# Attention outputs from rotated, transposed operands in the edge stage of a graph, attention and expert layer

## The reference, cut to what matters

```python
# gnn: edges (row, col), 4 heads of 64
e = leaky_relu(a_src.Wh[row] + a_dst.Wh[col], 0.2); e = exp(e - max(e))
h_new = segment_sum(Wh[col] * e / segment_sum(e)[row], row) + Wh
# mix: qn, kn are normalised; v1 = [1, v]
kv_mod = einsum('bhni,bhnj,bhne->bhije', kn, kn, v1/N)
kv = einsum('bhnd,bhne->bhde', kn, v1/N)
y = 0.5*einsum('bhni,bhnj,bhije->bhne', qn, qn, kv_mod) + s2*einsum('bhnd,bhde->bhne', qn, kv) + s4*vsum
out = (y[..., 1:] / y[..., :1]) @ Wproj.T + bproj
```

## Time and profile before

| | |
|---|---|
| Time, median of 3 | 3498.43 us (3497.71 to 3507.61) |
| Span of the profiled execution | 4552.4 us; no time of its own is given beside the span |
| Instructions | 80191 |
| Busy share of that span | PE 68%, DVE 61%, ACT 43%, POOL 47% |
| Transfers | 452.9 MB, mean 99 GB/s |

### The profile page before, as it was taken

The page is one execution under the profiler, slowest core; times in us unless marked ns, Lnnn a source line. Parts: engine busy times, 40 slices in busy tenths (PEclk is TensorE's granted clock), DMA queues, the critical chain, the costliest instruction groups (busy, mean ns, idle before and its releaser), DMA issues.

```text
span 4552.4 us, 80191 instructions
## 1 busy us (share of the span) xinstructions
PE 3118.0 (68%) x17657; PEld 2176.0 (48%) x17657; DVE 2760.2 (61%) x6376; ACT 1951.9 (43%) x5742; POOL 2159.7 (47%) x2438
## 2 busy tenths in 40 slices
PE   4888266666666666667777777777776444777895
PEld 2333133333333333456555555555555333666785
DVE  8999866666666666656555555565555465434322
ACT  4777133333333333344444444444444222544674
POOL 5877455455555555544444444444444532123123
PEclk8888677777887877788888888888888776988998
DMA  2222244343434434433333333333333333334344
GB/s 67 99 96 89 89 103 103 106 103 101 110 100 104 121 99 105 110 89 90 84 92 81 87 89 83 83 87 85 84 88 83 94 112 130 105 109 150 96 136 134
DMA packets 326431, 452.92 MB, mean 99 GB/s; under 512 B 79020, under 2 KB 261482, under 8 KB 326052
## 3 DMA queue, kind: packets, MB, share of 16 engines
q0 software_dynamic: 85552, 236.37, 19.0%
q1 hardware_dynamic: 217896, 194.32, 14.9%
q10 hardware_dynamic: 22860, 20.83, 1.6%
HBM read 366.49 MB, written 84.82 MB: 99 GB/s over the span
## 4 chain that ended last, share of the span: by engine, by line
PE 27%; DVE 21%; issue 20%; another core or an unknown queue 15%; DVEq 7%; ACT 5%; POOL 3%; ACTq 1%; DMA 1%; SPq 1%; POOLq 0%
PE bank L2046 8%; PE bank L2230 4%; PE bank L2242 4%; DVE room L1582 3%; PE bank L2080 3%; DVE room L1374 2%; DVEq L1541 2%; PE bank L2091 2%; DVE room L1373 2%; DVE room L1565 2%; DVE room L1535 1%; DVE room L1555 1%; PE bank L2055 1%; ACT room L1175 1%
## 5 line engine op out<-in xcount | busy, mean ns | idle before, releaser
L884 POOL DMA_INDIRECT room<-table,room x1564 | 1504.4, 962 | 1594.4 <-DVE room L1565 1127.9
L2046 PE MATMUL bank<-room 128*128 128x260 f32 x3520 | 1053.1, 449 | 472.4 <-DVE room L1565 291.2
L2046 PEld LDWEIGHTS bank<-room 128*128 128x128 f32 x3520 | 752.3, 225 | 634.4 <-issue 510.2
L1565 DVE TENSOR_TENSOR room<-room,bank 128x1024 f32<-128x1024 f32 x440 | 534.3, 1214 | 71.3 <-issue 41.1
L1582 DVE TENSOR_TENSOR room<-bank,room 128x1024 f32<-128x1024 f32 x392 | 477.5, 1218 | 162.6 <-remote 88.9
L1175 ACT ACTIVATE room<-bank 128x512 f32<-128x512 f32 (+1 forms) x588 | 252.4, 487 | 393.0 <-remote 306.0
L1555 DVE TENSOR_REDUCE room<-bank 128x32 f32<-128x128 f32 x440 | 125.2, 285 | 426.9 <-remote 263.8
L1107 ACT ACTIVATE bank<-room 128x16 f32<-128x16 f32 x440 | 80.8, 184 | 671.8 <-DVE room L1559 432.9
L1100 ACT ACTIVATE spare<-away,ones 128x512 bf16<-128x512 bf16 x440 | 317.6, 722 | 57.3 <-ACT away L1097 7.6
L2080 PE MATMUL bank<-ident,room 128*128 128x128 f32 x1764 | 298.8, 325 | 22.3 <-issue 11.1
L1115 ACT ACTIVATE bank<-room 128x96 f32<-128x96 f32 x392 | 96.4, 246 | 506.5 <-DVE room L1585 331.5
(11 more groups left out here) (321 smaller groups left out, 5010.7 us busy)
## 6 DMA issues: line engine op xcount, KB each, us to landing
spare<-rows_dram SPq DMA_DIRECT2D x440, 128.0 KB
room<-table,room POOLq DMA_INDIRECT x1564
kv_dram<-room SPq DMA_DIRECT2D x49, 324.0 KB, 2.2
room<-kv_dram SPq DMA_DIRECT2D x196, 81.0 KB
y_dram<-planes SPq DMA_DIRECT2D x119, 128.0 KB
room<-xs_dram ACTq DMA_DIRECT2D x110, 128.0 KB
q_dram<-room SPq DMA_DIRECT2D x49, 192.0 KB, 1.9
room<-q_dram SPq DMA_DIRECT2D x196, 48.0 KB
```

The source lines that it names most:

```text
L884: pool.indirect_dma_start(G[:, k.slot, u, :], None, table, bass.IndirectOffsetOnAxis(ap=ixbuf[:, k.slot, u:u + 1].bitcast(I32), axis=0)).t ...
L1565: dve.tensor_tensor(Gw[:, h, :, 0:C].rearrange("p u (h d) -> p u h d", h=GH), G[:, bass.ds(slot, 1), :, 0:C].rearrange("p a u (h d) -> p ( ...
L2046: ins = pe.matmul(pbank[1 + h][:, 0:TW], OH[:, s, u, :], Gw[:, h, u, :], start=(u == 0), stop=(u == U - 1))
```

## The change: what it does, and the diff

1. **q is stored transposed.** In stage 1 PE transposes q of tile a-2 (`turn_q`, three 128x128 transposes, after `project(a)`), ACT copies it (`copy_qt`, 256 and 128 columns), SP stores 192 KB into `qt_dram` (384 rows x 6272 tokens) instead of `q_dram`.
2. **q laps work on 512 tokens.** Thirteen groups of four laps (52 laps, the last group has one tile of 128 tokens). A lap handles one pair of heads for 512 tokens, a step two of a head's four chunks of 128 features. SP loads for each head q transposed four times (`rot_a`, 4 x 32 rows) and shifted by each distance (`rot_b`, 4 x 32 x 4 rows of 2 KB): 8 transfers and 1.25 MB per head; and per lap six transfers of 256 KB in all for the tail. DVE multiplies 2 x 512 columns per step, both inputs in SBUF, and once per lap the tail (512). The product is already what `y_part` needs: PE runs two matmuls of 512 columns per step, and one for the tail per lap. `ft_part`, `q_part`, `copy_unit` for q, and the two small feature operations for q go. The rest of the chain (`tail_part`, `normalise_y`, `add_bias`, `store_mix`) runs per token tile as before, one group later.
3. **Row scores of four steps at once.** PE `row_scores(lap)` makes them for a lap, two laps ahead, in bank 3; DVE `take_scores` reduces 512 elements once per lap into `row_sum`, in place of a reduction of 128 and an ordering wait per step. ACT's `copy_oht` runs eight steps ahead, SP's row loads one lap further ahead.
4. `one_hot` reads `iota_ps` (now bank 4) in all laps. `feat` and `feat_tail` have four buffers. `w2` is loaded by SP after the last q lap, `zeros` is cleared after the edge stage. GpSimd has more to clear before the edge stage (`ysT` 4096 elements per partition, `tail_y` 512, `tail_x` 1024 and two selects over it); its gathers are unchanged.

```diff
@@ sync: stores of stage 1 @@
-            sp.dma_start(q_dram[rows, :], qs[:, a.slot, :]).then_inc(st_out[a.slot], 16)
+        def store_qt(a):
+            sp.wait_ge(qt_copied, a.n + 1)
+            sp.dma_start(qt_dram.rearrange("(b p) n -> p b n", p=P)[:, :, bass.ds(a.n * P, P)], qts[:, a.slot, :, :]).then_inc(st_out[a.slot], 16)
...
@@ sync: loads of the q laps @@
+        def load_rot(gq, h):
+            r, w = h % 2, width(gq)
+            n = 8 * gq + h
+            if not isinstance(n, int) or n >= 2:
+                sp.wait_ge(qf_done, 2 * n - 2)
+            tok = bass.ds(gq * QW, w)
+            for d in range(4):
+                sp.dma_start(rot_a[d * MD:(d + 1) * MD, r, 0:w], qt_dram[h * XD:h * XD + MD, tok]).then_inc(unit_loaded[r], 16)
+                rows = bass.AP(qt_dram.tensor, qt_dram.offset + (h * XD + d) * NP, [[NP, MD], [4 * NP, FCH], [1, NP]])
+                sp.dma_start(rot_b[d * MD:(d + 1) * MD, r, :, 0:w], rows[:, :, tok]).then_inc(unit_loaded[r], 16)
...
+        def q_group(gq):
+            for l in range(QG):
+                n = 4 * gq + l
+                for s in range(4):
+                    load_row(At(n + (LAPS_K + 2), s, 4))
+                    if s == 0:
+                        load_tail(gq, l)
+                    if s % 2 == 0:
+                        load_rot(gq, 2 * l + s // 2)
+                    if s == 1 and (not isinstance(n, int) or n >= 7):
+                        store_mix(n - 7)
...
+        sp.wait_ge(y_step, 16 * NQG)
+        for e in range(XE):
+            sp.dma_start(w2[:, e, :, :], t["W2"][e].rearrange("(c p) n -> p c n", p=P)).then_inc(s_w4e, 16)
@@ scalar @@
+        def copy_qt(a):
...
+            act.activation(qts[:, s, 0:2, :].rearrange("p b n -> p (b n)"), pbank[0][:, 2 * P:4 * P], ACT.Copy)
+            act.activation(qts[:, s, 2, :], pbank[4 + (s + 1) % 2][:, MH * V1:MH * V1 + P], ACT.Copy).then_inc(qt_copied, 1)
...
-                if (k + 3).inside(STEPS):
-                    copy_oht(k + 3)
+                if (k + 8).inside(STEPS):
+                    if s < 3:
+                        copy_oht(k + 8)
+                    if s == 2:
+                        copy_oht(k + 9)
@@ vector @@
+        def take_scores(lap):
+            dve.wait_ge(s_made, lap + 1)
+            if not isinstance(lap, int) or lap > 0:
+                dve.wait_ge(z_done, 4 * lap)
+            dve.tensor_reduce(row_sum[:, :].rearrange("p (u n) -> p u n", n=2 * GH),
+                              score_ps[:, :].rearrange("p (u j n) -> p u n j", j=4, n=2 * GH), AX.X, ALU.add).then_inc(scores_taken, 1)
...
-            o.then(dve.tensor_reduce(ps, parts, AX.X, ALU.add))
...
+        def q_features(gq, l, s):
+            w, n = width(gq), 16 * gq + 4 * l + s
+            h, r = 2 * l + s // 2, (s // 2) % 2
+            if s == 0:
+                dve.wait_ge(unit_loaded[2], 16 * ((KL - 1) * PAIRS + T_LOADS * (4 * gq + l + 1)))
+                x = tail_x[:, l % 2, 0:w]
+                dve.tensor_tensor(x, x, tail_y[:, 0:w], ALU.mult).then_inc(qtail_done, 1)
+            dve.wait_ge(unit_loaded[r], 16 * ((KL if r == 0 else KL - 1) * PAIRS + R_LOADS * (4 * gq + l + 1)))
...
+            c = 2 * (s % 2)
+            dve.tensor_tensor(feat[:, s, :, 0:w], rot_a[:, r, 0:w].unsqueeze(1).to_broadcast([P, 2, w]),
+                              rot_b[:, r, c:c + 2, 0:w], ALU.mult).then_inc(qf_done, 1)
@@ tensor @@
+        def turn_q(a):
+            s = a.slot % 2
+            pe.wait_ge(qkn_done, a.n + 1)
+            for b in range(QB):
+                out = pbank[0][:, (2 + b) * P:(3 + b) * P] if b < 2 else pbank[4 + (s + 1) % 2][:, MH * V1:MH * V1 + P]
+                ins = pe.transpose(out, qs[:, s, b * P:(b + 1) * P], ident[:])
+            ins.then_inc(qt_made, 1)
...
+        def y_part(gq, l, s):
...
+            pe.wait_ge(qf_done, n + 1)
+            for j in range(2):
+                c = 2 * (s % 2) + j
+                ins = pe.matmul(out[p0:p0 + V1, :], kvm[:, h, c, :], feat[:, s, j, 0:w],
+                                start=False, stop=(c == FCH - 1), skip_group_check=True)
+            ins.then_inc(y_step, 1)
...
                 sum_rows(k)
-                if (k + 2).inside(STEPS):
-                    row_scores(k + 2)
                 if extra is not None:
                     extra(s)
+                if s == 3 and (k + 8).inside(STEPS):
+                    row_scores(i + 2)
```

More of the change, by code:

```diff
@@ L244, in _build @@
     half = carve(NORMS)
+    qts = carve(2, QB, P)
     assert used[0] <= PLAN_AT, used[0]
@@ L276, in _build @@
     ixbuf = carve(4, U)
+    rot_a = carve(2, QW)
+    assert used[0] <= PLAN_AT, used[0]
+    used[0] = edge_at
+    OH = carve(4, U, P)
+    feat = carve(4, 2, MAIN)
+    rot_b = carve(2, FCH, QW)
     stage3_end = used[0]
@@ L1134, in next_k, with lap @@
             return copy
-        def next_q(q):
-            def copy(s):
-                if s < 3 or not isinstance(q, int) or q < NT - 1:
-                    copy_q(q + (s + 1) // 4, (s + 1) % 4)
-            return copy
-        def lap(i, mode="", q=None, unit=None):
+        def lap(i, unit=None, after=None):
             for s in range(4):
@@ L1181, in _, with q_after, after, q_group @@
-        for s in range(3):
+        def q_after(gq, l, b):
+            n = 4 * gq + l
+            def after():
+                if l > 0:
+                    copy_yst(gq, l - 1, b)
+                elif not isinstance(gq, int) or gq > 0:
+                    copy_yst(gq - 1, QG - 1, 1 - b)
+                if not isinstance(n, int) or 5 <= n < NT + 5:
+                    copy_yt(n - 5)
+            return after
+        def q_group(gq, b):
+            for l in range(QG):
+                lap(4 * gq + (LAPS_K + l), after=q_after(gq, l, b))
@@ L1184, in _ @@
         exps(At(0, 0, 4))
+        for s in range(4):
+            copy_oht(At(1, s, 4))
         PER = 8
@@ L1203, in _ @@
             act.sem_inc(kvt_copied, 1)
-        lap(LAPS_K, "q", 0, next_q(0))
+        q_group(0, 0)
+        q_group(1, 1)
         base = o.count
-        with act.Fori(1, NT - 1) as q:
-            o.laps(q - 1, base, PER + 2)
-            lap(q + LAPS_K, "q", q, next_q(q))
-        o.count = base + (PER + 2) * (NT - 2)
-        lap(LAPS_K + NT - 1, "q", NT - 1, next_q(NT - 1))
-        copy_yst(NT - 1)
-        act.wait_ge(yt_made, NT)
-        copy_yt()
-        base = o.count
-        with act.Fori(LAPS_K + NT, LAPS - 1) as i:
-            o.laps(i - (LAPS_K + NT), base, PER)
+        per = 2 * QG * (PER + 2)
+        with act.Fori(1, NQG // 2) as i:
+            o.laps(i - 1, base, per)
+            q_group(2 * i, 0)
+            q_group(2 * i + 1, 1)
+        o.count = base + per * (NQG // 2 - 1)
+        q_group(NQG - 1, 0)
+        lap(LAPS_Q, after=q_after(NQG, 0, 1))
+        lap(LAPS_Q + 1, after=lambda: copy_yt(NT - 1))
+        for i in range(LAPS_Q + 2, LAPS):
             lap(i)
-        o.count = base + PER * (LAPS - 1 - LAPS_K - NT)
-        lap(LAPS - 1)
         act.wait_ge(den_done, STEPS)
@@ L1631, in lap @@
                     scores(k + 1, slot, need)
+                if s == 2 and (k + 4).inside(STEPS):
+                    take_scores(i + 1)
                 if k.after(1):
@@ L1972, in project @@
                 out = (qk_bank(a) if bank == 2 else pbank[bank + s])[:, 0:width]
+                if bank == 4 and a.after(3):
+                    pe.wait_ge(qt_copied, a.n - 2)
                 for c in range(2):
```

374 lines of the change are left out of this document (200 added, 174 removed).

## The result

The changed kernel takes 3694.7 us (median of 4, 3689.9 to 3706.4) against 3500.5 for the kernel before in the same session: ratio 1.056, 95% interval 1.054 to 1.058. Forecast were 3365 us and a range up to 3500.

A forecast was written before the change was run, and what follows sets the result against it. VectorE was taken to bound k laps (19.3 us), VectorE and TensorE handing over work q laps (21.2). 3498.4 - 57 - 96 - 2 + 12 + 8 + 1 = 3364 us, predicted as 3365, range 3290 to 3500.

The forecast's parts named there:

- before the first lap (12 + 8 + 1): Added cost: 12 us for stage 1's q transposes, 8 for ScalarE's early one-hots, 1 for GpSimd's extra clearing.
- 52 k laps: Row scores at once lighten VectorE to 17.6 us; GpSimd then bounds the lap at 18.2, saving 57 us.
- 48 q laps: Lighter TensorE and VectorE work, 0.5 added for handing over: lap from 21.2 to 19.2 us, saving 96 us.
- last ten laps: The 49th q lap and three edge laps (75.5 us) become four quarter-width laps (73): 2 us saved.
- the transfers' term: q laps move 5.4 MB instead of 2.7; at 318 GB/s that takes 17.0 us per lap, hidden.
- Rival 3: q loads to 32 partitions run at half rate; VectorE waits at its product, gathers land late: 24 us laps, 3596; chance 0.09.
- signs of being wrong: Profile after: VectorE waiting for rot_a or rot_b, hundreds of gathers over 1.2 us, or over 20 us of stage-1 waits.
- rival 2: VectorE's two-SBUF-input products hold GpSimd each step: 4.3 us more, 22.4 per q lap, 3520 total; chance 0.09.
- Rival 1: Transfers bound the q laps at 261 GB/s: 20.7 us per lap, 3438 total; chance 0.17.
- Rival 5: q laps were bound by something that stays; only the k laps gain, 3462 us; chance 0.04.
- rival 4: GpSimd's gathers are not at 5.10 us in timed runs: k laps 17.6, q laps 18.9, 3320 total; chance 0.11.
- "`w2` loads at the end have six laps to land: 0": Moving the w2 loads after the last q lap costs nothing, 0 us.

The follow-up runs named there:

- b0_before: The kernel before, unchanged, run again for an unstretched profile; 3500.1 us.
- e3_noload: Changed kernel without any q loads of heads after the first two; 3430.8 us, ratio 0.980.
- e5_stride: Changed kernel with each 32-partition q load going to every fourth partition instead of 32 in a row; 3433 us, one run.
- e7_psum: e3_noload with the q product's first input taken from PSUM in place of rot_a; 3391 us, one run.
- e9_store: Changed kernel with loads to every fourth partition, sums reordered to match, output stores between row loads, w2 from the last lap but one; 3438.6 us, ratio 0.982.
- e1_wide: Changed kernel with a head's q loads as five transfers filling all 128 partitions instead of eight to 32, same bytes and packets; 3484.9 us, ratio 0.995.
- e4_order: As e1_wide, but partitions distance-major, so each transfer's outermost count is 4 instead of 32; 4222 us, ratio 1.206.

## Why the prediction was wrong

Lengths from the windows above, against b0_before. The last ten laps before are taken as one mean q lap and nine: 21.1 + 159.3.

| term | forecast, us | changed kernel | e3_noload |
|---|---|---|---|
| before the first lap (12 + 8 + 1) | +21 | +8 | +11 |
| 52 k laps | -57 | -51 | -57 |
| 48 q laps | -96 | +223 | -50 |
| last ten laps | -2 | +14 | +12 |
| stage 4 | 0 | +4 | +9 |
| sum | -134 | +197 | -73 |

The 49th q lap of the kernel before took 27.5 us, not 21.1. With the laps as they stand in its trace its last ten took 186.7 us; then the changed kernel lost 229 us in 48 q laps and 8 in the last ten, and the sum stays.

**The step that failed** is the transfers' term: "New packets are 2 KB, longer than those of the q window, so I take 318, 17.0, which is hidden". The bytes were right (259 MB in 48 laps, 5.4 MB per lap), the rate was not. It was 210 GB/s at a share of 0.93, 25.7 us per lap, and the old gathers waited in it. With the loads spread the rate over the share is 265/0.88 = 301 GB/s (e5_stride), 17.9 us for 5.4 MB: the 318 was near the truth for loads over all partitions, and what it left out is where the new ones land. The rate was chosen by the length of packets, "longer than those of the q window". That holds for most of them by count, but not by bytes: by the packet records 22,336 packets of 4160 bytes carry 93 of the 134 MB in the q laps of b0_before. And no row showed a packet going to 32 partitions in a row.

Rival 3 said that such loads are slow, at half the rate, with 24 us per lap and 3596 us. It had a chance of 0.09, though the working had nothing against it but the depth of two heads. Its price was low by 1.7 us per lap, and made up otherwise. By the packet records the 2 KB packets took 13.1 us of each engine's time per lap, not 18 (in e5_stride 8.6). All others took 10.9, not 6: gathers 7.6 (e5_stride 6.6, before 7.0), and the rest mostly row numbers. The gathers' packets went from 161 ns (e3_noload) to 255 in the median, but only from 252 to 268 in the mean. And its first sign, VectorE waiting at its product, did not come. The gathers were late, as it also said.

Of the signs of being wrong the one that nearly came, 98 gathers of over 1.2 us, pointed to rival 2, and e5_stride has 94 of them at 20.36 us per lap. The list of signs named `rot_a` and `rot_b` alone; with the DMA engines over 0.9 busy every transfer is a candidate, the one with least lead first.

**Rival 1** (the upper bound by the q window, 20.7) was near to what the spread loads gave, 20.36, but for another reason: e3_noload had 20.06 without them. **Rival 2** was right in kind and small in size: 0.5 us per lap by e7_psum, not the 4.3 of its full price. **Rival 5** fell: without its loads the q lap lost 1 us.

**The k laps** went as worked out. VectorE's part of a step without `take_scores` is, by the changed kernel's timeline,

```profile
899.53 1.21 DVE L1653 TENSOR_TENSOR room<-room,bank 128x1024 f32<-128x1024 f32 x1
...
902.03 0.17 DVE L1644 TENSOR_TENSOR room<-room 128x16 f32<-128x16 f32 x1
...
903.68 1.21 DVE L1653 TENSOR_TENSOR room<-room,bank 128x1024 f32<-128x1024 f32 x1
```

4.15 us in place of the 4.82 of the earlier trace rows; four of them and 0.69 for the reduction of 512 (0.68 forecast) are 17.3, and the median lap is 17.5. The mean, 18.4, is GpSimd's: between 560 and 1490 us it waited only 1.5 us for a buffer, and its groups start 5.09 us apart in the median, in an execution as long as the timed ones, which also refutes **rival 4**. Forecast were 17.6 and 18.2.

**The q laps without transfers** were 20.06, 0.9 over the forecast 19.2. The holding took the whole 0.5 that was added for it and for handing over (0.52 by e7_psum). VectorE's own lap came out longer, 19.5 in e7_psum where 18.7 was summed. It was busy there for 837/48 = 17.4 us per lap and idle for 2.1, more than the sum held; of these 100 us in all, the two largest waits are for its own result before L1644 (26 us) and for the exponentials before L1653 (16 us), and the rest is in small pieces.

**Before the first lap**: 6 to 12 us in all kernels with the change, where 21 were forecast. VectorE's wait for ScalarE before the sums of squares in stage 1 was 3.9 us, as little as before (3.8 in the earlier trace rows), so the 12 of stage 1 did not show at VectorE; the rest was not taken apart. **"`w2` loads at the end have six laps to land: 0"** looked at the wrong end: they landed in time, but stood ahead of a store. The lap of that wait took 35.5 us, 21.3 before; e9_store's last ten laps, 186.1 us, are level with the 186.7 before. **The lower end of the range**, 3290, is not what its words give: rival 4 with the 12 of stage 1 at nothing is 3308, and 3299 with the 8 and the 1 at nothing too. The 3 to 10 us more in stage 4 were not examined; the clearing of `zeros` now lies there.

Open: how much of the loss is TensorE's lower granted clock (0.91 in the q laps, 0.99 in e5_stride), which came and went with the loads. Open too: why e1_wide (five transfers of 256 KB to all partitions) is 0.85 us per lap slower than e5_stride (four of 64 and four of 256 KB). It was not tried.

## What to carry to other kernels

Cost a transfer by the partitions it lands on, not by bytes and packet length alone: in full q laps 32 or 64 partitions in a row took 152 to 156 ns per 2 KB packet where 128, or 32 spread four apart, took 84, and an outermost count of 4 kept the engines half idle. When a change fills the DMA engines, look for the damage at the transfer with the least lead, here an old gather, not at the new loads. And give a rival that no row excludes more than a small chance.

## What the runs showed of the hardware that was not expected

- The place of the destination partitions alone, at equal bytes, packets, transfers and queue, made 3695 or 3433 us (the changed kernel and e5_stride).
- Beside the narrow loads the gathers' packets were slower too, 255 ns in the median and 268 in the mean, against 161 and 234 beside the spread ones.
- The order of two counts in an access pattern, 4 x 32 in place of 32 x 4, cost 737 us (e4_order against e1_wide), with the DMA engines half idle.
- TensorE's granted clock was 0.99 of 2.4 GHz in the q laps of e5_stride, 0.91 in those of the changed kernel and 0.78 in those of e4_order, so the last two had stretches at 1.2 GHz.
